# Edge keys decoded one turn ahead of their gather, with four buffers for indices and segment masks

## The chip, the cores and the metric

The kernel runs on one core of a Trainium2 chip. The metric is device time of the whole kernel in microseconds. Engines are named as in the profile: PE (TensorE), DVE (VectorE), ACT (ScalarE), POOL (GpSimd), SP (SyncE).

## The reference

The input is a batch of images, 128 channels of 32 x 32, that is 32768 tokens of 128 values for each of two halves. A convolution block with binarised weights comes first. Then a graph attention layer over 524288 random edges plus one self edge for each token sets the gates of a mixture of four experts:

```
h = (x_flat @ W_gat).reshape(M, HEADS, NUM_EXPERTS)          # 4 heads, 4 experts
e = leaky_relu(a_src[src] + a_dst[dst], 0.2)
ee = exp(e - segment_max(e, dst)[dst]);  denom = segment_sum(ee, dst)
agg = segment_sum(h[src] * (ee / denom[dst])[:, :, None], dst)
... layernorm, mean over heads, top 2 of 4, softmax ...
out = sum over experts of gate * (gelu(x @ W1[ei] + b1[ei]) @ W2[ei] + b2[ei])
```

What matters here is the middle: for every edge one row `h[src]` of 24 floats has to be fetched, and maxima, sums and products have to be run along edges sorted by their destination.

## The kernel before

The kernel has four stages, one after the other: `sorter` sorts the edges by destination (the first 1078 us, on DVE), `mixer` does the convolution block and writes the rows of `h` to memory, `attention` walks the sorted edges, and `finish_lower` collects the sums for each token and finishes the first half of the images. The change is in `attention` alone.

`attention` lays the 557056 sorted entries out as 128 partitions of 4352 and walks them in `CHUNKS` = 64 chunks of `COLS` = 68 columns. Five engines run the same loop, `rounds(eng, 6, LAST, 3, 4, body)`, over 65 turns k; each calls its own `body(k, at, turn)`, and semaphores alone keep them in step. `at` is the turn's number within the unrolled loop, so that `at % 2` and `at % 4` name buffers.

One turn k of DVE, in program order (DVE works strictly in this order):

1. Decode of chunk k (L788 to L811): it waits for the key load, splits the packed keys into a segment number `seg`, the source row `index` (L799; after it `idx` is signalled, L800) and three masks `start`, `cont`, `cut`. Before L799 it waits (L798) until the gather of chunk k-2 has landed, because `index` has two buffers. Each instruction waits for the one before (`go`).
2. In turns 0 to 3 a quarter of the expert gates of the other half, `x.weigh_vector` (L814; its instructions are at L1113 to L1150), and in turn 0 also `x.start_vector`.
3. Four small instructions that split the targets for a histogram (L821 to L825).
4. Attend to chunk k-1 (L843 to L872): it waits for the gather of chunk k-1 (`gat`, L843). The first part (L848 to L862) makes the running maximum and the differences `dif`; ACT takes their exponentials (L770); the second part (L864 and 20 scans at L870) makes the running sums `out`, and signals `out` (L872).
5. The experts' share (`Experts.vector`, L1336): the output of the tile before (L1345), and then eight steps, each one product with the gate (`ex_hs`, L1351) and one group of 8 column pairs for the histogram: `one_hot` (L876 to L881) writes `is_lo` (L879) and `is_hi` (L880), 16 instructions a group, 128 a turn.

POOL, turn k (L735 to L740): it waits for `idx` of chunk k and for `out` of chunk k-2 (the buffer `got` has two places), and then issues 68 gathers (indirect DMAs), one for each column, 128 rows of 96 bytes each.

PE, turn k (`Experts.tensor`, L1284): 16 steps. In the first eight it multiplies `ex_hs` with the second weights (L1296), makes the next hidden values (L1250) and then the histogram matmuls of that step's group (L751), for which it waits on `one_hot`. The last eight steps are the other half's tile (`ex_kept_ps`, L1301), for which nothing of DVE is needed. ACT makes the GELUs (L1332) and the copies of the kept outputs (L1324) in the same order; the exponentials of turn k+1 (L770) come after all of them in ACT's program.

SP, turn k: it stores `out` of chunk k-1 (L713, after `out`), loads the keys (L718, after the decode of chunk k) and targets of chunk k+2, and moves the experts' tiles.

What orders the work around the change is therefore the program order of DVE, and two semaphores on POOL:

```
need(pool, S["idx"], k + 1)      # L735: indices of chunk k
need(pool, S["out"], k - 1)      # L736: sums of chunk k-2
```

Of the kernel before, what the change touches and what calls it, by code (L numbers as in the profile page):

```python
# [666 lines left out]
def attention(nc, edges_d, keys_d, rows_d, res_d, agg, half, gathers, make_experts=None, finish=None):  # L667
    with ExitStack() as ctx, ExitStack() as during:
        def keep(name, shape, dt=F32): return ctx.enter_context(nc.sbuf_tensor(f"e{half}_{name}", shape, dt))
        def sb(name, shape, dt=F32): return during.enter_context(nc.sbuf_tensor(f"e{half}_{name}", shape, dt))  # L670
# [24 lines left out]
        def decodes(k): return not isinstance(k, int) or k < CHUNKS  # L695
# [6 lines left out]
        with nc.Block() as block:  # L702
# [24 lines left out]
            @block.gpsimd  # L727
            def _(pool):
                pool.iota(iota_i[:, :], [[1, HIS]], base=0, channel_multiplier=0).then_inc(S["iot"], 1)
                if x: x.start_gpsimd(pool)  # L730
                pool.wait_ge(S["edge"], 1)
                pool.indirect_dma_start(head0[:, :], None, rows_d, bass.IndirectOffsetOnAxis(ap=first[:, :], axis=0)).then_inc(S["head"], 16)
                def body(k, at, turn):
                    if decodes(k):
                        need(pool, S["idx"], k + 1)  # L735
                        need(pool, S["out"], k - 1)  # L736
                        pool.sem_inc(S["free"], 1)
                        for c in range(COLS):
# [36 lines left out]
            def _(v):  # L775
                v.wait_ge(S["iot"], 1)
                v.tensor_copy(iota_f[:, :], iota_i[:, :]).then_inc(S["iot"], 1)
                v.tensor_copy(iota_b[:, :], iota_i[:, :]).then_inc(S["iot"], 1)

                def body(k, at, turn):  # L780
                    if decodes(k):
                        u = at % 2
                        i = [0]
                        def go(ins):
                            i[0] += 1
                            ins.then_inc(S["dec"], 1)
                            v.wait_ge(S["dec"], DEC * k + i[0])
                        v.wait_ge(S["key%d" % u], 16 * (at // 2 + 1) + 32 * turn)  # L788
                        kk = key[:, u, :]
                        go(v.tensor_scalar(sgn[:, :], kk, 31, None, ALU.arith_shift_right))  # L790
                        go(v.tensor_tensor(mag[:, :], kk, sgn[:, :], ALU.bitwise_xor))
                        go(v.tensor_scalar(low[:, :], mag[:, :], 16, None, ALU.logical_shift_right))
                        go(v.scalar_tensor_tensor(out=seg[:, :], in0=sgn[:, :], scalar=float(FLIP), in1=low[:, :], op0=ALU.mult, op1=ALU.add))
                        go(v.tensor_scalar(dfull[:, :], seg[:, :], float(SHIFT + HALF * half), None, ALU.add))
                        go(v.tensor_tensor(mag[:, :], mag[:, :], dfull[:, :], ALU.bitwise_xor))
# [5 lines left out]
                        go(v.tensor_tensor(start[:, u, :], seg[:, 1:COLS+1], seg[:, 0:COLS], ALU.not_equal))  # L801
                        go(v.tensor_scalar(cont[:, u, :], start[:, u, :], -1.0, 1.0, ALU.mult, ALU.add))
                        go(v.tensor_scalar(cut[:, u, :], start[:, u, :], -BIG, None, ALU.mult))
                        if isinstance(k, int) and k == 0:
                            go(v.tensor_copy(prev_seg[:, :], seg[:, 0:1]))
                            go(v.tensor_copy(first_seg[:, :], seg[:, 1:2]))
                            v.tensor_scalar(first[:, :], dfull[:, 1:2], 65535, None, ALU.bitwise_and).then_inc(S["edge"], 1)
                        else:
                            go(v.tensor_copy(last_seg[:, :], seg[:, COLS:COLS+1]))
                            go(v.tensor_copy(last_seg[:, :], seg[:, COLS:COLS+1]))  # L810
                        assert i[0] == DEC  # L811

                        if x and isinstance(k, int) and k < x.WEIGHINGS:
# [14 lines left out]
                    if attends(k):  # L828
                        q = (at - 1) % 2
                        j = k - 1  # L830
# [4 lines left out]
                        def settle():  # L835
                            v.wait_ge(S["proc"], PROC * j + i[0])
# [10 lines left out]
                        by_head = lambda ap: ap.unsqueeze(1).broadcast_to([P, HEADS, COLS])  # L847
                        go(v.tensor_tensor(adv[:, :, :], g[:, :, 20:24].rearrange("p c h -> p h c"), by_head(start[:, q, :]), ALU.mult)); settle()  # L848
                        for h in range(HEADS):
                            go(v.tensor_tensor_scan(ad[:, q, h, :], cont[:, q, :], adv[:, h, :], ad[:, 1 - q, h, COLS-1:COLS], ALU.mult, ALU.add))  # L850
                        settle()
# [3 lines left out]
                        for h in range(HEADS):  # L855
                            go(v.tensor_tensor_scan(mx[:, q, h, 1:COLS+1], cut[:, q, :], e[:, h, :], mx[:, 1 - q, h, COLS:COLS+1], ALU.add, ALU.max))
                        settle()
                        go(v.tensor_tensor(dif[:, 0, :, :], mx[:, q, :, 0:COLS], by_head(cut[:, q, :]), ALU.add)); settle()
                        go(v.tensor_tensor(dif[:, 0, :, :], dif[:, 0, :, :], mx[:, q, :, 1:COLS+1], ALU.subtract))
# [6 lines left out]
                        for h in range(HEADS):  # L866
                            for w in range(EXPERTS + 1):
                                ch = h * EXPERTS + w if w < EXPERTS else HEADS * EXPERTS + h
                                data = wgt[:, h, w, :] if w < EXPERTS else rp[:, 1, h, :]
                                go(v.tensor_tensor_scan(out[:, q, :, ch], rp[:, 0, h, :], data, out[:, 1 - q, COLS-1, ch:ch+1], ALU.mult, ALU.add))  # L870
# [748 lines left out]
```

## Time and profile before

| | us |
|---|---|
| median of 3 runs | 10095.95 (10090.94 to 10100.3) |
| span of the profiled execution | 10069.6 |
| median minus span (launch and end, and the spread of runs) | 26.4 |

| engine | busy us | share |
|---|---|---|
| DVE | 5609.3 | 56% |
| POOL | 5042.1 | 50% |
| PE | 4088.4 | 41% |
| ACT | 1868.9 | 19% |

The profiled execution stands for itself: its span is the time from its first to its last instruction, and the 26.4 us are what the median of the timed runs has beyond it. The profile is one execution's; a row of it gives an engine, a line of the kernel, an operation, the tiles it writes and reads, and times. `attention` takes the span from about 2132 to 9454 us, so it is nearly three quarters of the kernel.

### The profile page before, as it was taken

Reading aid. Unit: us, or ns where it says so; the run is one execution under the profiler, and the core shown is the slowest. Engines: PE = TensorE matmul, PEld = TensorE weight load, DVE = VectorE, ACT = ScalarE, POOL = GpSimd, SP = SyncE. Lnnn points to the kernel's source line nnn. Section 1 sums busy time; section 2 is a strip of 40 time slices with the busy share of each in tenths; the row PEclk is TensorE's granted clock in tenths of the full one; section 3 lists DMA queues with packets and bytes.
Section 4 is the critical chain, followed back from the end, with each engine's and each line's share of the span. In section 5 each row is a group of like instructions: output and inputs, shape, how many; then the busy total and the mean of one; then the engine's idle time right before and its main releaser. Section 6 shows DMA issues by size and latency. Waiting matters only on the chain. (4 is left out here: it accounts for less than half of the span.)

```text
span 10069.6 us, 67922 instructions
## 1 busy us (share of the span) xinstructions
PE 4088.4 (41%) x14109; PEld 1997.0 (20%) x14171; DVE 5609.3 (56%) x16515; ACT 1868.9 (19%) x3239; POOL 5042.1 (50%) x4836
## 2 busy tenths in 40 slices
PE   0011388833344444434444444344444444334233
PEld 0010255521111111112111111111111121111100
DVE  9999788845444444444444444444444444444388
ACT  0000377721111111111111111111111111111111
POOL 0000155545566556665656556665666556665452
PEclk9855688866676777677776777667776777667655
DMA  0000133311111111111111111111111111111156
GB/s 17 0 0 0 55 120 118 120 46 31 31 44 32 31 31 36 39 32 31 32 43 32 31 31 35 40 32 31 31 44 32 31 31 35 40 32 27 44 191 199
DMA packets 351386, 467.68 MB, mean 46 GB/s; under 512 B 176559, under 2 KB 252290, under 8 KB 334338
## 3 DMA queue, kind: packets, MB, share of 16 engines
q1 hardware_dynamic: 203562, 408.25, 11.6%
q0 software_dynamic: 147552, 56.95, 5.9%
q14 instruction: 241, 1.97, 0.1%
q8 instruction: 31, 0.51, 0.0%
HBM read 234.91 MB, written 229.93 MB: 46 GB/s over the span
## 5 line engine op out<-in xcount | busy, mean ns | idle before, releaser
L739 POOL DMA_INDIRECT e_got<-rows,e_index x4352 | 4285.0, 985 | 2982.4 <-DVEq L800 1674.8
L751 PE MATMUL e_count_ps<-e_is_hi,e_is_lo 128*128 128x256 bf16 x4096 | 699.1, 328 | 3044.3 <-DMA keys<-s_u_b 2348.6
L879 DVE TENSOR_SCALAR e_is_lo<-e_iota_b,e_tlo 128x128 bf16<-128x128 bf16 x4096 | 1057.3, 258 | 1534.1 <-issue 1174.2
L880 DVE TENSOR_SCALAR e_is_hi<-e_iota_b,e_thi 128x256 bf16<-128x256 bf16 x4096 | 1184.2, 290 | 1247.4 <-issue 1247.2
L1332 ACT ACTIVATE ex_hh<-ex_hid_ps,ex_b 128x512 f32<-128x512 f32 x1024 | 696.7, 687 | 5889.8 <-remote 2776.9
L751 PEld LDWEIGHTS e_count_ps<-e_is_hi,e_is_lo 128*128 128x128 bf16 x4096 | 426.0, 114 | 3391.5 <-DMA keys<-s_u_b 2419.4
L1296 PE MATMUL ex_out_ps<-ex_hs,ex_w 128*128 128x512 f32 x1024 | 757.8, 832 | 18.1 <-remote 11.4
L1250 PE MATMUL ex_hid_ps<-ex_tn,ex_w 128*128 128x512 f32 x1024 | 661.3, 734 | 0.0
L1301 PE MATMUL ex_kept_ps<-ex_hh,ex_w 128*128 128x512 f32 x1024 | 542.1, 611 | 273.2 <-ACT ex_kept L1324 187.4
L864 DVE TENSOR_TENSOR e_wgt<-e_got,e_rp 128x1088 f32<-128x1088 f32 x64 | 180.5, 2820 | 681.1 <-issue 499.9
L180 POOL MEMSET m_identb<- 128x128 bf16 x1 | 0.2, 205 | 1077.7 <-POOLq L85 1077.7
L1250 PE MATMUL ex_hid_ps<-ex_lower,ex_w 128*128 128x512 f32 x1024 | 522.9, 592 | 0.0
L1351 DVE TENSOR_TENSOR ex_hs<-ex_hh,ex_gate_ps 128x512 f32<-128x512 f32 x512 | 348.3, 680 | 171.3 <-issue 169.4
L1291 PE MATMUL ex_out_ps<-ex_turned,ex_b 36*128 36x512 bf16 x64 | 38.5, 601 | 891.4 <-DVE ex_o L1345 454.8
L384 ACT ACTIVATE m_xt<-m_ln_ps,m_nb,m_rs 128x128 f32<-128x128 f32 x1024 | 370.6, 466 | 31.6 <-DVE m_nb L326 31.6
L1470 POOL DMA_INDIRECT c_trow<-sums,c_tidx x256 | 260.2, 1017 | 188.9 <-DVE c_tidx L1520 96.1
L1250 PEld LDWEIGHTS ex_hid_ps<-ex_tn,ex_w 128*128 128x128 f32 x1024 | 260.9, 255 | 377.6 <-issue 372.4
L207 POOL TENSOR_TENSOR m_xm<-m_out,m_xin 128x1024 f32<-128x1024 f32 x64 | 151.4, 2366 | 362.5 <-issue 303.4
L654 PE MATMUL s_turned<-s_ident,s_ping 128*128 128x128 f32 x288 | 54.9, 379 | 674.8 <-DVEq L546 674.8
L235 PE MATMUL m_conv_ps<-m_sg,m_w1T 128*128 128x512 bf16 x1152 | 318.8, 439 | 5.9 <-DVE m_z L349 5.9
L870 DVE TENSOR_TENSOR_SCAN e_out<-e_rp,e_out,e_wgt 128x68 f32<-128x68 f32 x1024 | 289.8, 364 | 28.2 <-issue 24.1
L1301 PEld LDWEIGHTS ex_kept_ps<-ex_hh,ex_w 128*128 128x128 f32 x1024 | 173.7, 189 | 554.5 <-ACT ex_hh L1332 284.2
(358 smaller groups left out, 6435.0 us busy)
## 6 DMA issues: line engine op xcount, KB each, us to landing
e_got<-rows,e_index POOLq DMA_INDIRECT x4352
kept<-ex_kept SPq DMA_DIRECT2D x64, 1024.0 KB
c_kept<-kept SPq DMA_DIRECT2D x64, 1024.0 KB
sums<-e_out SPq DMA_DIRECT2D x64, 816.0 KB
m_xin<-in_x_dram SPq DMA_DIRECT2D x64, 512.0 KB, 4.6
mid<-m_xm SPq DMA_DIRECT2D x64, 512.0 KB, 2.9
norm<-m_tn SPq DMA_DIRECT2D x64, 512.0 KB, 4.7
ex_tn<-norm SPq DMA_DIRECT2D x64, 256.0 KB
```

The costliest lines, as they stand in the source:

```text
L235: last = pe.matmul(conv_ps[:, hf*512:(hf+1)*512], w1T[:, t, :], sg1[:, at % 2, hf*rows_of+dy:hf*rows_of+dy+rows_of, dx:dx+W], start=(t == ...
L384: last = act.activation(xt[:, b*P:(b+1)*P], src[:, b*P:(b+1)*P], ACT.Identity, bias=nb[:, b:b+1], scale=rs[:, b:b+1])
L739: pool.indirect_dma_start(got[:, at % 2, c, :], None, rows_d, bass.IndirectOffsetOnAxis(ap=index[:, at % 2, c:c+1], axis=0)).then_inc(S["g ...
L751: last = pe.matmul(count_ps[:, 0:HIS], is_lo[:, g % 2, t, :], is_hi[:, g % 2, t, :], start=(isinstance(k, int) and k == 0 and g == 0 and t ...
L870: go(v.tensor_tensor_scan(out[:, q, :, ch], rp[:, 0, h, :], data, out[:, 1 - q, COLS-1, ch:ch+1], ALU.mult, ALU.add))
L879: v.tensor_scalar(is_lo[:, g % 2, t, :], iota_b[:, 0:P], tlo[:, n:n+1], None, ALU.is_equal)
L880: last = v.tensor_scalar(is_hi[:, g % 2, t, :], iota_b[:, :], thi[:, n:n+1], None, ALU.is_equal)
L1250: pe.matmul(self.hid_ps[:, s % 2, :], self.w1[:, e, f*P:(f+1)*P], tokens[:, at % 4, :], start=True, stop=True).then_inc(S["w1"], 1)
L1296: pe.matmul(self.out_ps[:, :], self.w2[:, e, f, :], self.hs[:, s % 2, :], start=False, stop=(s == self.GATED - 1)).then_inc(S["w2"], 1)
L1301: pe.matmul(self.kept_ps[:, :], self.w2[:, e, f, :], self.hh[:, s % 2, :], start=(f == 0), stop=(f == HID - 1)).then_inc(S["w2"], 1)
L1332: act.activation(self.hh[:, s % 2, :], self.hid_ps[:, s % 2, :], ACT.Gelu, bias=self.b1[:, s % self.GATED // HID, s % HID:s % HID + 1]).th ...
L1351: v.tensor_tensor(self.hs[:, s % 2, :], self.hh[:, s % 2, :], self.gate_ps[:, (s // HID) % 2, :], ALU.mult).then_inc(S["mul"], 1)
```

## The change

The decode becomes a function `decode(k, at, turn)`. It is called once before the loop for chunk 0, and then at the head of turn k for chunk k+1. `index`, `start`, `cont` and `cut` get four buffers (`at % 4`); the wait of the decode for the gather of chunk k-2 is gone. POOL's gather reads `index[:, at % 4, ...]`, and the attending part reads the masks of its own chunk, k-1. A loop variable `w` is renamed `lane`. Nothing else changes: not POOL's two waits, nor the order of steps 2 to 5 on DVE.

```diff
-        index = sb("index", [P, 2, COLS], I32); first = sb("first", [P, 1], I32)
-        start = sb("start", [P, 2, COLS]); cont = sb("cont", [P, 2, COLS]); cut = sb("cut", [P, 2, COLS])
+        index = sb("index", [P, 4, COLS], I32); first = sb("first", [P, 1], I32)
+        start = sb("start", [P, 4, COLS]); cont = sb("cont", [P, 4, COLS]); cut = sb("cut", [P, 4, COLS])
...
-                                bass.IndirectOffsetOnAxis(ap=index[:, at % 2, c:c+1], axis=0)).then_inc(S["gat%d" % (at % 4)], 16)
+                                bass.IndirectOffsetOnAxis(ap=index[:, at % 4, c:c+1], axis=0)).then_inc(S["gat%d" % (at % 4)], 16)
...
+                def decode(k, at, turn):
+                    u, w = at % 2, at % 4
...
+                    v.wait_ge(S["key%d" % u], 16 * (at // 2 + 1) + 32 * turn)
...
+                    go(v.tensor_scalar(index[:, w, :], mag[:, 1:COLS+1], 65535, None, ALU.bitwise_and))
+                    v.sem_inc(S["idx"], 1)
+                    go(v.tensor_tensor(start[:, w, :], seg[:, 1:COLS+1], seg[:, 0:COLS], ALU.not_equal))
+                    go(v.tensor_scalar(cont[:, w, :], start[:, w, :], -1.0, 1.0, ALU.mult, ALU.add))
+                    go(v.tensor_scalar(cut[:, w, :], start[:, w, :], -BIG, None, ALU.mult))
...
+                decode(0, 0, 0)
                 def body(k, at, turn):
+                    if not isinstance(k, int) or k + 1 < CHUNKS:
+                        decode(k + 1, at + 1, turn)
                     if decodes(k):
                         u = at % 2
...
-                        if not isinstance(k, int) or k >= 2:
-                            v.wait_ge(S["gat%d" % ((at - 2) % 4)], 16 * COLS * ((at - 2) // 4 + 1) + 16 * COLS * turn)
-                        go(v.tensor_scalar(index[:, u, :], mag[:, 1:COLS+1], 65535, None, ALU.bitwise_and))
-                        v.sem_inc(S["idx"], 1)
...
-                        q = (at - 1) % 2
+                        q, w = (at - 1) % 2, (at - 1) % 4
...
-                        go(v.tensor_tensor(adv[:, :, :], g[:, :, 20:24].rearrange("p c h -> p h c"), by_head(start[:, q, :]), ALU.mult)); settle()
+                        go(v.tensor_tensor(adv[:, :, :], g[:, :, 20:24].rearrange("p c h -> p h c"), by_head(start[:, w, :]), ALU.mult)); settle()
```

## Rows read from the trace of the kernel before

**Rows 1.** The page, parts 1 and 5: busy time by engine; the gathers.
```profile
PE 4088.4 (41%) x14109; PEld 1997.0 (20%) x14171; DVE 5609.3 (56%) x16515; ACT 1868.9 (19%) x3239; POOL 5042.1 (50%) x4836
...
L739 POOL DMA_INDIRECT e_got<-rows,e_index x4352 | 4285.0, 985 | 2982.4 <-DVEq L800 1674.8
```

**Rows 2.** Waits of POOL: total us, times, longest.
```profile
POOL e_got L739 <- DVEq L800: 1674.8, 63, 39.9
```

**Rows 3.** One turn cut into stretches: length, busy us of each engine, clock, DMA.
```profile
4552.10:4556.20 4.10, 3.93 (x16) 2.14 (x16) 3.24 (x18) 0.96 (x2) 1.19 (x2) 1.00 0.00 0
4556.20:4574.00 17.80, 11.64 (x26) 4.31 (x24) 6.13 (x16) 7.81 (x12) 13.60 (x14) 1.00 0.10 10
4574.00:4582.30 8.30, 0.00 (x0) 0.00 (x0) 7.97 (x21) 2.54 (x3) 7.01 (x5) 0.60 0.07 7
4582.30:4590.30 8.00, 7.22 (x17) 2.89 (x18) 7.25 (x32) 0.69 (x1) 6.17 (x7) 0.57 0.64 210
4590.30:4643.00 52.70, 13.07 (x32) 5.10 (x30) 12.41 (x39) 1.37 (x2) 39.73 (x43) 0.62 0.17 37
4643.00:4650.90 7.90, 3.49 (x11) 2.08 (x12) 0.00 (x0) 0.00 (x0) 0.00 (x0) 0.51 0.02 2
4650.90:4665.50 14.60, 12.16 (x49) 6.04 (x48) 13.69 (x68) 3.44 (x5) 0.00 (x0) 0.88 0.00 1
```

**Rows 4.** Timeline of that turn: first gather; end of ACT's tile; second attending part.
```profile
4554.71 0.95 POOL L739 DMA_INDIRECT e_got<-rows,e_index  x1 [27.30 <-DVEq L800]
...
4571.31 0.69 ACT L1324 ACTIVATE ex_kept<-ex_kept_ps,ex_b2c 128x512 f32<-128x512 f32 x1 [3.00 <-issue]
...
4574.00 2.82 DVE L864 TENSOR_TENSOR e_wgt<-e_got,e_rp 128x1088 f32<-128x1088 f32 x1 [10.96 <-ACT e_rp L770]
4574.07 3.49 POOL L739 DMA_INDIRECT e_got<-rows,e_index  x1 [0.30 <-issue]
...
4582.34 0.69 DVE L1345 TENSOR_TENSOR ex_o<-ex_xm,ex_out_ps 128x512 f32<-128x512 f32 x1 [0.33 <-DVE e_out L870]
```

**Rows 5.** Timeline later in that turn: two one-hots; a group's end, and PE's answer.
```profile
4608.86 0.28 DVE L880 TENSOR_SCALAR e_is_hi<-e_iota_b,e_thi 128x256 bf16<-128x256 bf16 x1 [1.03 <-issue]
4610.26 0.25 DVE L879 TENSOR_SCALAR e_is_lo<-e_iota_b,e_tlo 128x128 bf16<-128x128 bf16 x1 [1.11 <-issue]
...
4638.26 0.29 DVE L880 TENSOR_SCALAR e_is_hi<-e_iota_b,e_thi 128x256 bf16<-128x256 bf16 x1 [1.14 <-issue]
...
4647.41 1.89 PE L751 MATMUL e_count_ps<-e_is_hi,e_is_lo 128*128 128x256 bf16 x8 [17.38 <-DMA keys<-s_u_b]
```

**Rows 6.** Gather starts (turns 0, 1, 21, finish) up to DVE's slowing, columns as rows 3.
```profile
2137.70:2164.00 26.30, 0.00 (x0) 0.00 (x0) 21.11 (x45) 4.61 (x5) 20.07 (x21) 0.50 0.11 10
2255.90:2290.60 34.70, 13.23 (x29) 4.89 (x28) 20.97 (x37) 9.88 (x14) 26.41 (x28) 0.82 0.09 9
4554.70:4590.30 35.60, 20.36 (x46) 7.77 (x45) 22.45 (x75) 11.72 (x16) 27.97 (x26) 0.81 0.21 54
9495.60:9587.00 91.40, 0.00 (x0) 0.00 (x0) 15.11 (x39) 2.65 (x3) 69.00 (x72) 0.50 0.22 62
```

**Rows 7.** Timeline of turn 2: attending late beside a gather, first and last.
```profile
2428.27 0.82 DVE L848 TENSOR_TENSOR e_adv<-e_got,e_start 128x272 f32<-128x272 f32 x1 [2.50 <-DMA s_u_a<-keys]
...
2476.78 0.69 DVE L1345 TENSOR_TENSOR ex_o<-ex_xm,ex_out_ps 128x512 f32<-128x512 f32 x1 [6.84 <-remote]
```

**Rows 8.** Timeline of turn 1: the gates' first and last instruction.
```profile
2256.34 1.22 DVE L1113 TENSOR_TENSOR ex_cen<-agg,ex_con 128x1024 f32<-128x1024 f32 x1
...
2294.82 0.56 DVE L1150 COPY parts<-parts 128x768 bf16<-128x768 bf16 x1 [1.04 <-DVE parts L1150]
```

**Rows 9.** Lines L790, L1345, L879: durations ns, first and last start.
```profile
L790 DVE TENSOR_SCALAR e_sgn<-e_key x64: 178/183/200, 2132.1 to 9314.4; 128x69 int32<-128x69 int32 x64
L1345 DVE TENSOR_TENSOR ex_o<-ex_xm,ex_out_ps x64: 686/687/690, 2351.7 to 9454.1; 128x512 f32<-128x512 f32 x64
L879 DVE TENSOR_SCALAR e_is_lo<-e_iota_b,e_tlo x4096: 233/247/504, 2195.2 to 9424.6; 128x128 bf16<-128x128 bf16 x196
```

More of the change, by code:

```diff
@@ L778, in _, with go @@
                 v.tensor_copy(iota_b[:, :], iota_i[:, :]).then_inc(S["iot"], 1)
+                def decode(k, at, turn):
+                    u, w = at % 2, at % 4
+                    i = [0]
+                    def go(ins):
+                        i[0] += 1
+                        ins.then_inc(S["dec"], 1)
+                        v.wait_ge(S["dec"], DEC * k + i[0])
+                    v.wait_ge(S["key%d" % u], 16 * (at // 2 + 1) + 32 * turn)
+                    kk = key[:, u, :]
+                    go(v.tensor_scalar(sgn[:, :], kk, 31, None, ALU.arith_shift_right))
+                    go(v.tensor_tensor(mag[:, :], kk, sgn[:, :], ALU.bitwise_xor))
+                    go(v.tensor_scalar(low[:, :], mag[:, :], 16, None, ALU.logical_shift_right))
+                    go(v.scalar_tensor_tensor(out=seg[:, :], in0=sgn[:, :], scalar=float(FLIP), in1=low[:, :], op0=ALU.mult, op1=ALU.add))
+                    go(v.tensor_scalar(dfull[:, :], seg[:, :], float(SHIFT + HALF * half), None, ALU.add))
+                    go(v.tensor_tensor(mag[:, :], mag[:, :], dfull[:, :], ALU.bitwise_xor))
+                    go(v.tensor_scalar(index[:, w, :], mag[:, 1:COLS+1], 65535, None, ALU.bitwise_and))
[3 more added lines that the diff above has]
+                    go(v.tensor_scalar(cut[:, w, :], start[:, w, :], -BIG, None, ALU.mult))
+                    if isinstance(k, int) and k == 0:
+                        go(v.tensor_copy(prev_seg[:, :], seg[:, 0:1]))
+                        go(v.tensor_copy(first_seg[:, :], seg[:, 1:2]))
+                        v.tensor_scalar(first[:, :], dfull[:, 1:2], 65535, None, ALU.bitwise_and).then_inc(S["edge"], 1)
+                    else:
+                        go(v.tensor_copy(last_seg[:, :], seg[:, COLS:COLS+1]))
+                        go(v.tensor_copy(last_seg[:, :], seg[:, COLS:COLS+1]))
+                    assert i[0] == DEC
@@ L780, in body @@
+                decode(0, 0, 0)
                 def body(k, at, turn):
+                    if not isinstance(k, int) or k + 1 < CHUNKS:
+                        decode(k + 1, at + 1, turn)
                     if decodes(k):
                         u = at % 2
[L783 to L794, printed above, removed]
@@ L795, in body @@
-                        go(v.tensor_tensor(mag[:, :], mag[:, :], dfull[:, :], ALU.bitwise_xor))
-                        if not isinstance(k, int) or k >= 2:
-                            v.wait_ge(S["gat%d" % ((at - 2) % 4)], 16 * COLS * ((at - 2) // 4 + 1) + 16 * COLS * turn)
-                        go(v.tensor_scalar(index[:, u, :], mag[:, 1:COLS+1], 65535, None, ALU.bitwise_and))
-                        v.sem_inc(S["idx"], 1)
-                        go(v.tensor_tensor(start[:, u, :], seg[:, 1:COLS+1], seg[:, 0:COLS], ALU.not_equal))
@@ L802, in body @@
[L802 to L810, printed above, removed]
@@ L811, in body @@
-                        assert i[0] == DEC
                         if x and isinstance(k, int) and k < x.WEIGHINGS:
@@ L847, in body @@
                         by_head = lambda ap: ap.unsqueeze(1).broadcast_to([P, HEADS, COLS])
-                        go(v.tensor_tensor(adv[:, :, :], g[:, :, 20:24].rearrange("p c h -> p h c"), by_head(start[:, q, :]), ALU.mult)); settle()
+                        go(v.tensor_tensor(adv[:, :, :], g[:, :, 20:24].rearrange("p c h -> p h c"), by_head(start[:, w, :]), ALU.mult)); settle()
                         for h in range(HEADS):
-                            go(v.tensor_tensor_scan(ad[:, q, h, :], cont[:, q, :], adv[:, h, :], ad[:, 1 - q, h, COLS-1:COLS], ALU.mult, ALU.add))
+                            go(v.tensor_tensor_scan(ad[:, q, h, :], cont[:, w, :], adv[:, h, :], ad[:, 1 - q, h, COLS-1:COLS], ALU.mult, ALU.add))
                         settle()
@@ L855, in body @@
                         for h in range(HEADS):
-                            go(v.tensor_tensor_scan(mx[:, q, h, 1:COLS+1], cut[:, q, :], e[:, h, :], mx[:, 1 - q, h, COLS:COLS+1], ALU.add, ALU.max))
+                            go(v.tensor_tensor_scan(mx[:, q, h, 1:COLS+1], cut[:, w, :], e[:, h, :], mx[:, 1 - q, h, COLS:COLS+1], ALU.add, ALU.max))
                         settle()
-                        go(v.tensor_tensor(dif[:, 0, :, :], mx[:, q, :, 0:COLS], by_head(cut[:, q, :]), ALU.add)); settle()
+                        go(v.tensor_tensor(dif[:, 0, :, :], mx[:, q, :, 0:COLS], by_head(cut[:, w, :]), ALU.add)); settle()
                         go(v.tensor_tensor(dif[:, 0, :, :], dif[:, 0, :, :], mx[:, q, :, 1:COLS+1], ALU.subtract))
@@ L866, in body @@
                         for h in range(HEADS):
-                            for w in range(EXPERTS + 1):
-                                ch = h * EXPERTS + w if w < EXPERTS else HEADS * EXPERTS + h
-                                data = wgt[:, h, w, :] if w < EXPERTS else rp[:, 1, h, :]
+                            for lane in range(EXPERTS + 1):
+                                ch = h * EXPERTS + lane if lane < EXPERTS else HEADS * EXPERTS + h
+                                data = wgt[:, h, lane, :] if lane < EXPERTS else rp[:, 1, h, :]
                                 go(v.tensor_tensor_scan(out[:, q, :, ch], rp[:, 0, h, :], data, out[:, 1 - q, COLS-1, ch:ch+1], ALU.mult, ALU.add))
```

## The prediction, as it stood before the result

> **What bounds the kernel now.** I read the page first. No engine is full: DVE is busy for 56% of the span and POOL for 50% [rows 1]. The largest single group is POOL's 4352 gathers, and ahead of them POOL stood idle for 1674.8 us, in 63 waits for the indices that DVE's decode signals [rows 1, 2]: 26.6 us a turn. That is what the change aims at. Whether it is worth anything depends on what DVE does while POOL gathers, so I cut one turn (chunk 21) into stretches [rows 3]. A turn is 113.4 us there, and DVE's program runs through it in order:
>
> - 4.1 us: decode and target split, 18 instructions.
> - 17.8 us: first attending part, of which 11.0 us are a wait for ACT's exponentials [rows 4]. ACT comes late because its half of the kept tile ends only at 4572.0, 20 us after DVE's last one-hot. So 6.8 us are work.
> - 8.3 us: second attending part. At its end `out` is signalled.
> - 83.2 us: the experts' share with the 128 one-hots, 139 instructions in all (32 + 39 + 0 + 68). This part I call H. At DVE's full rate (68 instructions in 13.69 us busy, 4.97 per us) it would take 28 us.
>
> The gather of a turn starts 2.6 us into it, at 4554.7, and ends at 4643, 88.3 us long. For its first 36 us DVE runs beside it at full rate: 32 instructions in 8.0 us between 4582.3 and 4590.3. Then something gives way: 39 instructions in 60.6 us, 1.55 us each, two neighbours 1.4 us apart though each is busy for 0.25 to 0.29 us, and PE sees the end of a group 8.9 us late (4638.55 to 4647.41) [rows 3, 5]. This lasts until 4650.9, 7.9 us after the last gather; then DVE is fast at once. So a turn is bounded by neither POOL nor DVE alone: gather start + 96 us of which 60 are nearly lost, and after it the 14.6 us of one-hots that are left, and only then the next decode and the next gather.
>
> **The change, part by part.** *Buffers and the wait that goes.* The wait for the gather of chunk k-2 never ended late: the attending part of turn k-1 had waited for that gather already. Worth 0. The renamed variable: 0.
>
> *The decode moved ahead.* The same 12 instructions, once a turn; one extra call before the loop. It needs the keys of chunk k+1 at the head of turn k. SP issues that load after `out` of turn k-1, as before, and H lies between, 28 us at the least; so 0, and SP passes no other queue. Queued behind the key wait on DVE would be the whole turn, but nothing makes it late.
>
> *When POOL starts.* Of its two waits, `idx` of chunk k is now there a turn early, and `out` of chunk k-2 becomes the one that ends last: it is signalled at the end of attending in turn k-1. The gather of chunk k thus starts at the head of H in turn k-1, not after the decode in turn k. POOL stays one gather in each turn, and its idle time does not go: it waits for `out` in place of `idx`.
>
> *What lies beside the gather.* Before: decode, attending with its 11 us wait, then H. Now: H first, then the next decode, then attending. Both orders have the same DVE work, so the question is how much of it is done before DVE slows. The onsets in the trace [rows 6]: 26.3 us after the gather's start in turn 0, 34.7 in turn 1, 35.6 in turn 21, but with 21.1, 21.0 and 22.5 us of DVE busy time in each. In the finishing stage 72 gathers ran in 91.4 us with 15.1 us of DVE and no slowing. I take 21 us of DVE work beside a gather as the allowance; DVE's waits do not use it up. By instructions (45, 37, 75) or by gathers (21, 28, 26) the same rows agree less well or not with the finishing stage; these are rivals below.
>
> Count from the gather's start T = 0, the head of H. 21 us at 4.97 per us: 104 of 139 instructions. The other 35 at 1.55 us: 54 us, T+75. The next decode, 18 instructions at 1.4 us, is 25 us, cut off where the slowing ends at T+96: done at T+97. First attending part 6.8 us: T+104. The exponentials need ACT's 20 us of kept tile, begun at T+75: if it runs at full rate there is no wait and attending ends at T+112, if it stands still until T+96 it ends at T+124. I take the middle and a little less, P = 115 us a turn, because PE and ACT post fewer signals than DVE. Before it is 113.4. The 11 us wait used to lie in the fast part of a gather and be covered by nothing else; what is saved of it is paid back by 12 us more of slow stretch (75 for 61 us).
>
> *The ends* [rows 7 to 9]. Turn 0: gathers 0 and 1 run back to back, 2 x 88 us, so the slowing lasts until about 188 us after the decode at 2132.1. H starts at 63 us (first one-hot 2195.2): 125/1.55 = 81 instructions, then 58 fast, 12 us: turn 0 takes 200 us. Turn 1 up to its `out`: 4.1 + 38.5 (gates, with their waits) + 6.8 + 8.3 = 58. Turns 2 and 3: 96 + 38.5 + 6.8 + 8.3 = 150 each. Then 60 turns of P. At the end H without a gather and one attending with its wait, 28 + 26 = 54. Sum 612 + 60 P. Before, from the first decode to the last L1345, it is 9454.1 - 2132.1 = 7322. With P = 115: 7512, so 190 us more; break-even is P = 111.8. The profiled span becomes 10260, and with the 26.4 us that the median has beyond the span, 10286 us.
>
> *A rule weighed.* Beside the 2.82 us product of two SBUF operands (L864) a gather took 3.49 us in place of 0.95, and it started first on neither side by more than 0.07 us [rows 4]; beside the fast one-hots gathers kept nearly their rate, 7 in 8.0 us, and DVE its own [rows 3]. The Trainium skill (SBUF — State Buffer, "Who interferes with whom") has one rule for both: VectorE and GpSimd share one port pair under an exclusive lock, so that a tensor_scalar in a two-port mode and a GpSimd instruction block each other fully. It speaks against this change, which puts all one-hots beside gathers. For L864 the trace agrees; for the one-hots it agrees from 4590 on at best and not in the 8 us before. By the rule every one-hot would be slow from the gather's start, which is the far end of rival A.
>
> **The rivals.**
>
> A. *The one-hots use up the allowance faster than their busy time, and H becomes the bound* (slower). They come at 4.97 per us, where the attending parts have about 2.6. If the allowance is a number of instructions, it is 37 to 75 [rows 6]: gone after 7 to 15 us. Then by T+96 52 to 57 more are done, 12 to 45 are left, H ends at T+98 to T+105, and decode, attending and the whole wait follow in the open, 30.2 us: P = 129 to 135. With none fast: 96/1.55 = 62 done, 77 left, 15.5 us, P = 142. It decides where fewer than about 85 of the 139 run before the onset. For it: the slowing is paid per instruction (1.4 us whatever its length). Against it: 37 against 75 is no constant. Time: 60 x 129 + 612 - 7322 = 1030 more, 11126; at 135, 11486.
>
> B. *The onset goes by gathers or by time, and H fits before it* (faster). 21 to 28 gathers are 26 to 35 us. H (28) and the decode (4) end at T+32; attending runs slowly, 48.5 us as in turn 2 [rows 7], so `out` comes at T+81 and the next gather starts at T+88, when POOL is free; with some of the next H beside the end of the old one P is about 95. If the onset is at 25 us, 15 instructions of H are slow (T+48), the decode (T+73), the first attending part, 21 us as in turn 2 up to L864, T+94, and the second is fast: P = 104. For it: 26.3 to 35.6 us is a narrow spread. Against it: the finishing stage, 72 gathers without onset. Time: 9090 to 9630.
>
> C. *The change doesn't do what it says*: `out` hides the early indices in a way that leaves the turn as it was, P = 112. Time 60 x 112 + 612 - 7322 = 10 more, 10106. Only the phase of the gather could spare it.
>
> **How the numbers follow.** The forecast 0.45 (P 110 to 120, its own range 9990 to 10590), A 0.22, B 0.30, C 0.03. A measurement tells about 0.2%, 20 us, from no change. Of the forecast's 0.45, 0.08 lies below 10076 (P under 111.5) and 0.04 within 20 us. Faster: 0.30 + 0.08 = 0.38. Same: 0.04 + 0.03 = 0.07. Slower: 0.33 + 0.22 = 0.55. The range leaves out the fast half of B with its price under 9500 and the far end of A over 11150, together about 2 in 10.
>
> **What would show it.** Right: POOL's wait ahead of L739 is no longer on L800 but on DVE's L872, still about 25 us a turn; the first gather of a turn starts within 1 us of L1345; one-hots are fast for about 20 us after it, then 1.4 us apart; L864 waits for ACT only briefly. Turn 0 is near 200 us. Wrong: a fast H to its end and slow scans at L870 (B), slow one-hots within 15 us of L1345 and L864 waiting 11 us (A), or two gathers without a gap in the steady turns.

## The result, and the profile after

The changed kernel takes 11572.6 us (median of 4 runs, 11562.8 to 11579.6) against 10094.1 us before on the same chip: ratio 1.146, 95% interval 1.1445 to 1.1478. It is slower by 1479 us, outside the range that was given.

The page of the changed kernel (busy time by engine; gathers; one-hots; the experts' activation) and three rows of its waits (total us, times, longest):

```profile
PE 4234.9 (37%) x14109; PEld 2062.7 (18%) x14171; DVE 5410.4 (47%) x16515; ACT 1860.6 (16%) x3239; POOL 4873.6 (42%) x4836
...
L739 POOL DMA_INDIRECT e_got<-rows,e_index x4352 | 4117.4, 946 | 4592.1 <-DVEq L875 3285.0
L882 DVE TENSOR_SCALAR e_is_lo<-e_iota_b,e_tlo 128x128 bf16<-128x128 bf16 x4096 | 1068.1, 261 | 2868.4 <-remote 2143.1
...
L1335 ACT ACTIVATE ex_hh<-ex_hid_ps,ex_b 128x512 f32<-128x512 f32 x1024 | 689.9, 686 | 7464.5 <-remote 4328.7
```
```profile
ACT ex_hh L1335 <- remote: 4328.7, 180, 36.5
POOL e_got L739 <- DVEq L875: 3285.0, 62, 87.7
DVE e_is_lo L882 <- remote: 2143.1, 160, 21.1
```

Beside [rows 1, 2]: POOL's wait has moved from the decode (1674.8 us) to the signal `out` (3285.0 us, 53 us each time). It did not go, it doubled. The largest wait on the list is ACT's, and it was so before the change as well, at two thirds of the size. The prediction did not read this row. Below it, from [rows 3]'s turn, ACT's longest idle time (its product was ready at 4605.80, PE's L1250):

```profile
ACT ex_hh L1332 <- remote: 2776.9, 130, 33.6
...
4631.36 0.69 ACT L1332 ACTIVATE ex_hh<-ex_hid_ps,ex_b 128x512 f32<-128x512 f32 x1 [32.90 <-remote]
```

One steady turn of the changed kernel from the first gather, cut as [rows 3]: to the end of the fast start; to the end of the slow stretch; rest of H; decode and target split; attending. Columns as there.

```profile
4746.90:4756.00 9.10, 8.74 (x24) 3.74 (x25) 9.10 (x44) 0.69 (x1) 6.91 (x8) 0.63 0.90 305
4756.00:4842.60 86.60, 17.90 (x51) 7.90 (x48) 12.00 (x47) 2.06 (x3) 57.31 (x61) 0.58 0.10 12
4842.60:4852.40 9.80, 6.76 (x24) 3.66 (x24) 9.78 (x50) 1.95 (x3) 0.00 (x0) 0.66 0.00 0
4852.40:4856.20 3.80, 3.80 (x16) 2.04 (x16) 3.04 (x17) 1.11 (x2) 0.00 (x0) 1.00 0.00 0
4856.20:4883.60 27.40, 12.34 (x27) 4.50 (x25) 14.73 (x39) 10.60 (x15) 0.04 (x1) 0.87 0.00 0
```

The turn is 136.7 us (113.4 in [rows 3]). The gather is no longer than before, 84.7 us. What has grown is the time without a gather, 52 us in place of 25: rest of H, decode, and all of attending lie in it. The time comes out of the prediction's own sum with this turn: 60 x 136.5 (the mean turn) + 612 - 7322 = 1480 us more.

What the slow stretch is made of stands in the timeline (start, length, instruction, idle time before it). These are the third product of the turn on PE, ready at 4758.17, ACT's step before it, free at 4759.18, ACT's answer to the product, and DVE's answer to ACT:

```profile
4757.15 1.02 PE L1253 MATMUL ex_hid_ps<-ex_tn,ex_w 128*128 128x512 f32 x2
...
4758.49 0.69 ACT L1335 ACTIVATE ex_hh<-ex_hid_ps,ex_b 128x512 f32<-128x512 f32 x1 [6.05 <-PE ex_hid_ps L1253]
...
4786.63 0.69 ACT L1335 ACTIVATE ex_hh<-ex_hid_ps,ex_b 128x512 f32<-128x512 f32 x1 [27.45 <-issue]
4790.05 0.69 DVE L1354 TENSOR_TENSOR ex_hs<-ex_hh,ex_gate_ps 128x512 f32<-128x512 f32 x1 [5.88 <-remote]
```

ACT stands idle for 27.45 us with product and buffer ready (the buffer's last reader on DVE was done at 4754.85) and nothing else to do; DVE starts 2.7 us after ACT's end. The turn's first product was ready at 4751.63, and ACT started at 4751.75. The profile puts most of these waits down to `remote` or `issue`, which names no engine, so the end of whatever an instruction needs has to be looked up in the timeline.

This can be done for every hand-over of H, in the turns whose H starts between 3000 and 8000 us. An instruction's lateness is its start minus the later of two times: when its engine was free, and when what it needs had ended. The longest, in us:
```
                           before  changed  e8 (below)
PE's product to ACT          27.4     36.5     40.6
PE's histogram to DVE        10.6     21.1     22.0
DVE's one-hots to PE         10.1     11.0      0.1
ACT's GELU to DVE             1.1      2.8      2.7
```
So the lateness goes by the producer. It is long behind PE, and behind DVE where DVE ran a group of 16 one-hots just before.

### The profile page after: what moved, and what is told of

Its sections match the earlier page's. It is cut to its first block and busy times, and to the rows that moved or that the text cites. A ratio compares the mean times of both kernels' runs of the same rounds, so it can differ in the third digit from the quotient of the medians.

```text
span 11561.1 us, 67889 instructions
## 1 busy us (share of the span) xinstructions
PE 4234.9 (37%) x14109; PEld 2062.7 (18%) x14171; DVE 5410.4 (47%) x16515; ACT 1860.6 (16%) x3239; POOL 4873.6 (42%) x4836
## 5 line engine op out<-in xcount | busy, mean ns | idle before, releaser
L739 POOL DMA_INDIRECT e_got<-rows,e_index x4352 | 4117.4, 946 | 4592.1 <-DVEq L875 3285.0
L751 PE MATMUL e_count_ps<-e_is_hi,e_is_lo 128*128 128x256 bf16 x4096 | 771.1, 352 | 4131.7 <-DMA keys<-s_u_b 1972.3
L751 PEld LDWEIGHTS e_count_ps<-e_is_hi,e_is_lo 128*128 128x128 bf16 x4096 | 463.2, 122 | 4533.7 <-DMA keys<-s_u_b 2008.6
L1299 PE MATMUL ex_out_ps<-ex_hs,ex_w 128*128 128x512 f32 x1024 | 819.7, 896 | 391.0 <-issue 262.2
L1253 PE MATMUL ex_hid_ps<-ex_lower,ex_w 128*128 128x512 f32 x1024 | 546.8, 616 | 0.0
L867 DVE TENSOR_TENSOR e_wgt<-e_got,e_rp 128x1088 f32<-128x1088 f32 x64 | 180.5, 2820 | 737.0 <-ACT e_rp L770 736.6
L1299 PEld LDWEIGHTS ex_out_ps<-ex_hs,ex_w 128*128 128x128 f32 x1024 | 227.9, 275 | 472.6 <-issue 283.7
L1241 DVE COPY ex_turned<-ex_turned_ps 36x512 bf16<-36x512 bf16 x64 | 26.7, 417 | 607.7 <-remote 480.0
```

The source lines that it names most:

```text
L751: last = pe.matmul(count_ps[:, 0:HIS], is_lo[:, g % 2, t, :], is_hi[:, g % 2, t, :], start=(isinstance(k, int) and k == 0 and g == 0 and t ...
L1253: pe.matmul(self.hid_ps[:, s % 2, :], self.w1[:, e, f*P:(f+1)*P], tokens[:, at % 4, :], start=True, stop=True).then_inc(S["w1"], 1)
L1299: pe.matmul(self.out_ps[:, :], self.w2[:, e, f, :], self.hs[:, s % 2, :], start=False, stop=(s == self.GATED - 1)).then_inc(S["w2"], 1)
```

## The experiments

Before on the same chip: 10027 us for e1 to e4, 10020 for e5 to e8, 10083 for e9 to e12, 10087 for e13 to e16, 10095 for e17 and e18. Ratios with 95% intervals; e8, e13, e14 are one run each, e2 to e4 two. T is the start of a turn's gathers.

**e1, the phase of the gather alone.** The decode stays a turn ahead, the gather starts where it did before.
```
 decode(k + 1, ...)              # head of turn k
+v.sem_inc(S["go"], 1)
 ...
+need(pool, S["go"], k + 1)      # POOL, ahead of chunk k's gathers
```


> The changed kernel with one more wait: POOL issues the gather of chunk k only after DVE has passed the head of turn k, just behind the decode of chunk k+1. So the decode stays a turn ahead and the four buffers stay, and only the start of the gather goes back to where it was. Theory PHASE (the loss comes from where in DVE's turn the gather lies, the one-hots now being at its head): the turn is 113 us again and the time 10050 to 10150. Rival BODY (the decode ahead, its code or its buffers cost by themselves): it stays near 11570.

10076 us, 1.0051 (1.0031 to 1.0071). So 14% of the 14.6% are the phase; decoding ahead with four buffers, with the added signal, costs 0.5%.

**e2, a phase between.** `go` is released ahead of the turn's sixth group of one-hots (`g == 5`).


> The changed kernel with the gather of chunk k+1 released inside the experts' share of turn k, behind its fifth group of one-hots: 48 one-hots lie at the head of the gather, then decode and attending. PHASE with an allowance of about 45 one-hot instructions (onset 9 to 11 us after the gather's start, as in the changed kernel): attending runs slowly, about 48 us, to T+64, then about 12 one-hots in 32 us, the rest after T+96: turn about 115, 10200. PHASE with an allowance by DVE busy time of 21 us: turn 105 to 107, about 9650. BODY: near 11570.

10671 us, 1.064 (turns of 112 to 132 us): above what either allowance gave (10200 and 9650) and well under BODY. The later in H the gather starts, the less is lost.

**e3, e4, another form of one-hot, changed order.** e3 reads `iota_f` in place of `iota_b`; e4 writes a group's 16 one-hots with two broadcast `tensor_tensor`.


> The changed kernel with the one-hots compared from the fp32 iota in place of the bf16 one; output, count and order of instructions are the same. Theory PORT (the slowing comes from the one-hots' bf16 mode, which takes something that the gathers need): the share with the one-hots takes about 40 us at full rate beside the gather, the turn falls to about the gather's 88 us, 8700 to 9200. Rival COUNT (each DVE instruction costs, whatever its mode): onset after about 45 instructions as before, turn 136 or a little more, 11550 to 11900.

> The changed kernel with the 16 one-hot instructions of a group made by two (8 columns at once by broadcast), the same elements written. COUNT: 34 instructions in the experts' share in place of 139, so it fits before the onset or loses little: turn 88 to 103, 8700 to 9650. A theory of DVE busy time (21 us): onset at the sixth group, turn about 103, 9650. PORT or a theory of written elements: the onset comes as early as now and the turn stays over 120, above 10600.

e3: 10617 us, 1.0586, between the ranges of PORT and COUNT. Every second H now ran fast to its end beside the gathers (139 instructions by T+35), which refutes both the allowance by instructions and the one by 21 us of busy time. The next H, behind two gathers in a row, was slow until 16 us after the last. e4: 10142 us, 1.0113, in no range of its three theories either (its H has 27 instructions, and not the 34 of the expectation). In both DVE holds POOL back. These are the first gathers of e3 beside float32 one-hots (1.48 and 1.54 us apart; in the changed kernel 1.25), and three of e4 beside the broadcast ones:

```profile
4607.82 0.94 POOL L739 DMA_INDIRECT e_got<-rows,e_index  x1 [0.30 <-issue]
4609.06 1.17 POOL L739 DMA_INDIRECT e_got<-rows,e_index  x1 [0.30 <-issue]
4610.54 1.23 POOL L739 DMA_INDIRECT e_got<-rows,e_index  x1 [0.30 <-issue]
4612.08 1.06 POOL L739 DMA_INDIRECT e_got<-rows,e_index  x1 [0.30 <-issue]
```
```profile
4597.72 3.95 POOL L739 DMA_INDIRECT e_got<-rows,e_index  x1 [0.30 <-issue]
4601.97 3.64 POOL L739 DMA_INDIRECT e_got<-rows,e_index  x1 [0.30 <-issue]
4605.91 3.67 POOL L739 DMA_INDIRECT e_got<-rows,e_index  x1 [0.30 <-issue]
```

I saw this only as a delay of POOL; that this may be what keeps H fast I saw only with e9.

**e5, SP's transfers.** SP waits for the end of H before it issues tile stores and loads.
```
-need(sp, S["fin"], k)
+need(sp, S["hdone"], k)         # DVE signals it after the last one-hot
```


> The changed kernel, but SP issues a token tile's output store, the next tile's three loads and the kept store only after the last one-hot of the turn (DVE signals it), not at the head of H; the sums store and the loads of keys and targets stay. In both kernels the time of the first slow one-hot also lies 8 to 9 us behind the start of SP's transfers (before: packets from 4582, onset at 4590; after: packets from 4747, onset at 4756), because both come with H. TRANSFERS (the SP transfers bring on the slow stretch): the one-hots stay fast to their end at about T+30, the onset moves behind the late transfers, period 95 to 115 us, time 9000 to 10300. ENGINES (it comes from DVE's own instructions beside the gathers): onset at T+9 to T+11 as before, H ends near T+105, period 134 to 140, time 11450 to 11750.

11464 us, 1.1442 (1.1423 to 1.1461), turns of 134 to 137 us: TRANSFERS is refuted.

**e6, e7, the other one-hots in the old order.** The edits of e4 and e3 on the kernel before.


> The kernel before, with each group's 16 one-hots as two broadcast tensor_tensor instructions (16 per turn in place of 128). PER-INSTRUCTION (what is lost in the slow stretch is 1.4 us an instruction): H of 27 instructions ends inside the gather, the turn is bounded by the gather plus decode, 2.6 + 88 + 3 to 10 us, period 94 to 105, time 9000 to 9700. PORT (the rate of DVE beside gathers is set by how long it works): the wide instructions carry the same elements, the turn stays 108 to 116, time 9800 to 10250.

> The kernel before, with one-hots that read the float32 iota in place of the bfloat16 one. Beside a gather's start the float32 one-hots of the changed order ran all 128 without slowing. FORM (bfloat16 one-hots bring the slow stretch on early): here the onset at 36 us after the gather's start goes away or moves past the end of H at about T+60, period 92 to 102, time 8800 to 9500. AGE (the slow stretch comes once gathers have run for 30 to 50 us with DVE busy): onset at T+36 to T+48 as before, period 105 to 116, time 9600 to 10250.

e6: 9934 us, 0.9916 (0.99 to 0.9933). e7: 10088 us, 1.0072, turns of 113.5 us on average, onset at T+33 to T+50. PER-INSTRUCTION and FORM are refuted: an eighth of the one-hots' instructions buys 0.8%, and the form nothing. Both times lie in the ranges of PORT and AGE, which had little change to forecast.

**e8, few one-hots.** `for t in range(RING)` becomes `range(1)` in the one-hots, after the first two groups of the first chunk.


> The changed kernel with only one pair of one-hots in each group in place of eight (16 per turn in place of 128; the other tiles keep what the first chunk left, so the counts are not the reference's). PER-INSTRUCTION: H of 27 instructions is done by about T+35 whatever its rate, the gathers go on without long gaps, period 85 to 105, time 8400 to 9700. If instead the period stays above 120, the 128 one-hots are not what the turn waits for, and PE's and ACT's late signals are.

11388 us, a turn of 133.8 us. This felled what the prediction and all experiments so far had taken for granted. One turn, first 9.1 us and slow stretch, then the fourth product of the turn on PE, ready at 4717.45, ACT's step before it, and its answer to the product; last, three starts on DVE and PE:

```profile
4703.90:4713.00 9.10, 8.78 (x28) 3.85 (x29) 3.40 (x11) 0.69 (x1) 6.96 (x8) 0.71 0.91 305
4713.00:4799.30 86.30, 17.32 (x54) 7.28 (x52) 3.97 (x11) 2.75 (x4) 57.30 (x61) 0.60 0.09 12
```
```profile
4716.43 1.02 PE L1253 MATMUL ex_hid_ps<-ex_tn,ex_w 128*128 128x512 f32 x2
...
4725.05 0.69 ACT L1335 ACTIVATE ex_hh<-ex_hid_ps,ex_b 128x512 f32<-128x512 f32 x1 [11.25 <-remote]
4759.34 0.69 ACT L1335 ACTIVATE ex_hh<-ex_hid_ps,ex_b 128x512 f32<-128x512 f32 x1 [33.61 <-remote]
```
```profile
4748.07 0.25 DVE L882 TENSOR_SCALAR e_is_lo<-e_iota_b,e_tlo 128x128 bf16<-128x128 bf16 x1 [19.61 <-remote]
...
4760.06 0.69 DVE L1354 TENSOR_TENSOR ex_hs<-ex_hh,ex_gate_ps 128x512 f32<-128x512 f32 x1 [11.44 <-issue]
...
4760.81 2.08 PE L1299 MATMUL ex_out_ps<-ex_hs,ex_w 128*128 128x512 f32 x2 [10.24 <-DVE ex_hs L1354]
```

DVE has 11 instructions in 86.3 us and the stretch is as long as with 47. So DVE's instructions are not what H waits for, but the hand-overs that go round PE, ACT and DVE eight times: here ACT answers PE's product 33.6 us after it was free, and DVE answers a group of PE's histogram, done at 4715.7, 19.6 us after it was free. The next hand-overs come without delay: ACT ends at 4760.03, DVE starts at 4760.06 and ends at 4760.75, PE starts at 4760.81. What is late comes from PE. A round of PE has 24 to 32 matmuls and weight loads, and e8 left them all. Whether a late hand-over costs time by the signal, or by the instructions that PE (or DVE, with 16 one-hots) ran before it, no run here tells: none changed PE's number.

**e9 to e12, room between the gathers.** One or two small instructions on POOL after each gather.
```
 pool.indirect_dma_start(...)
+for r in range(N):              # N = 1 (e9, e11) or 2 (e10, e12)
+    last = pool.memset(pause[:, c, r:r+1], 0.0)
 ...                             # last signals `rest`; POOL's next chunk waits for it
```


> The changed kernel with one 128x1 POOL memset after every gather, so that the gathers leave POOL about 1.41 us apart in place of 1.25. PACE (whatever serves the gathers behind POOL needs some 1.37 us for one, so at 1.25 us apart they pile up; signals of all engines then come late, until the pile is worked off: 8 us after one chunk of 68, 16 us after two chunks in a row, both 0.12 us a gather): at 1.41 us nothing piles up, the 8 rounds of H between PE, ACT and DVE take 30 to 35 us as they do at a gather's start, the gathers follow one another almost without a gap, 68 x 1.41 = 96 us, period 96 to 102, time 9050 to 9550. ENGINES (it comes from DVE's instructions beside any running gather): onset near T+10, the slow stretch longer because the gathers last 96 us, period 145 to 150, time 12000 to 12400.

> The same with two 128x1 memsets after every gather: about 1.57 us apart. PACE: no late signals either, period 68 x 1.57 = 107 to 112 us, time 9700 to 10100, so slower than with one memset. ENGINES: period 155 to 160, time 12600 to 13000.

> The kernel before with one 128x1 POOL memset after every gather. PACE: H runs fast, about 30 us, and ends near T+60, beside the gather; the next decode follows at once and POOL goes on without a gap, period 96 to 102, time 9050 to 9550. ENGINES: the turn is lengthened by the longer gather, 113 + 11 = 124 us, time 10700 to 10900.

> The kernel before with two memsets after every gather. PACE: period 107 to 112, time 9700 to 10100. ENGINES: 113 + 22 = 135 us, time 11300 to 11600.

Changed order: 11313 us (1.1225) and 10879 us (1.0786). Old order: 9812 us (0.973) and 9402 us (0.9323; 0.9307 to 0.9338). More work for POOL made both kernels faster, so ENGINES is refuted. PACE had the direction, and its range held in none of the four (e12 came out faster than it): the gathers were not evenly wider apart. POOL of e10, memsets between gathers, and one pause of 1.5 us:

```profile
4702.25 0.94 POOL L740 DMA_INDIRECT e_got<-rows,e_index  x1 [0.18 <-issue]
4703.19 0.11 POOL L743 MEMSET e_pause<- 128x1 f32 x1
4703.46 0.10 POOL L743 MEMSET e_pause<- 128x1 f32 x1 [0.16 <-issue]
4705.07 0.94 POOL L740 DMA_INDIRECT e_got<-rows,e_index  x1 [1.51 <-issue]
4706.02 0.14 POOL L743 MEMSET e_pause<- 128x1 f32 x2
4706.32 0.94 POOL L740 DMA_INDIRECT e_got<-rows,e_index  x1 [0.16 <-issue]
```

**e13, half the gathers.** `range(COLS)` becomes `range(COLS // 2)` on POOL from the third chunk on, and the counts waited for are halved.


> The changed kernel with 34 of a chunk's 68 gathers from the third chunk on (the other columns keep older rows, so its numbers are not the reference's). The gathers last 42.5 us in place of 85. BOUND TO THE END (H's signals stay late until some 10 us after the last gather, and then the last three rounds take 10 us): H ends near T+63, attending 31 us behind it, period 94, time 11560 - 60 x 42.5 = about 9010. BY ROUNDS (each of H's signals costs its time whatever is left of the gathers): H ends at T+75 or later, period 106 to 112, time 9700 to 10100. INSTRUCTIONS (the prediction's own arithmetic: 46 fast, the rest 1.55 us apart while it lasts): 46 + 28 = 74 by T+53, 65 left, 13 us: T+66, period 97, near the first.

8847 us, a turn of 92.4 us (9010 and 94 expected). Its four stretches, cut as in the changed kernel (fast start; slow; rest of H; decode and attending):

```profile
4748.30:4757.40 9.10, 8.79 (x23) 3.81 (x24) 9.10 (x44) 0.69 (x1) 6.96 (x8) 0.62 0.89 289
4757.40:4796.40 39.00, 9.22 (x34) 4.39 (x33) 7.92 (x29) 1.38 (x2) 25.22 (x27) 0.60 0.11 21
4796.40:4809.90 13.50, 12.39 (x44) 5.46 (x42) 13.50 (x68) 3.17 (x5) 0.00 (x0) 0.88 0.00 0
4809.90:4840.60 30.70, 15.57 (x40) 6.46 (x40) 17.68 (x55) 11.30 (x16) 0.00 (x0) 0.89 0.00 0
```

H ends at T+61.7, 19 us after the last gather; in the changed kernel at T+105.5, 21 us after it. That fits BOUND TO THE END and refutes BY ROUNDS: in these two kernels a turn is the length of its gathers and 50 to 52 us. INSTRUCTIONS (T+66, 97 us) lies only 5 us off; what speaks against it is e8. DVE was slow for 5.7 us after the last of 34 gathers, 9 to 11 after 68, 16 after 136 in a row (e3).

**e14 to e16, more room.** N = 4 in the changed order, N = 3 in the old one, N = 2 with the broadcast one-hots of e6.


> The changed kernel with four 128x1 memsets after each gather, about 1.65 us from gather to gather. With one H ended at T+101, with two at T+78. PACE: the signals are no longer late, H ends at T+35 to T+45, the gathers of 112 us follow one another with hardly a gap, period 112 to 116, time 10000 to 10250. ENGINES: the late signals stay, H ends near T+80 or later, period 140 and more, over 11600.

> The kernel before with three memsets after each gather, about 1.5 us from gather to gather. PACE: H ends beside the gather, period 68 x 1.5 = 102 to 106 us, time 9350 to 9600, about that of two memsets (9402), which ended 16 of 128 one-hots behind the gather. ENGINES: period over 110, time over 9800.

> The kernel before with two memsets after each gather and each group's one-hots as two broadcast instructions. Alone these took 6.8% and 0.8%. PACE: both shorten H beside the gather, the gathers (1.40 us apart) follow without a gap, period 96 to 101, time 9050 to 9350. If the broadcast instructions block POOL (they delayed gathers to 1.7 to 2.2 us apart), the gather becomes longer, period 103 to 110, time 9400 to 9800.

e14: 9179 us, 0.91 of before, under the range expected. e15: 9189 us, 0.9105 (0.909 to 0.9121), under its range too. e16: 9818 us, 0.9736, at the end of the range for gathers held up: the broadcast one-hots hold POOL up and take back more than half of what the pace gives. The gathers of e14 on the page, its longest wait for a signal, and a turn of 99.6 us from the start of H, which lies 15 us after the first gather (H and decode; wait for the gather; attending):

```profile
L740 POOL DMA_INDIRECT e_got<-rows,e_index x4352 | 4262.9, 980 | 907.1 <-issue 681.6
```
```profile
ACT ex_hh L1339 <- remote: 2756.2, 444, 12.3
```
```profile
4652.50:4702.20 49.70, 30.43 (x106) 14.06 (x107) 32.49 (x145) 4.81 (x7) 41.84 (x173) 0.81 0.25 70
4702.20:4736.90 34.70, 18.68 (x32) 6.80 (x30) 1.75 (x11) 8.52 (x12) 26.68 (x117) 0.75 0.08 9
4736.90:4752.10 15.20, 0.00 (x0) 0.00 (x0) 14.26 (x37) 3.21 (x4) 12.79 (x46) 0.61 0.07 8
```

All 139 instructions of H pass beside the gathers, ACT's tile too, and attending no longer waits for the exponentials. POOL goes from chunk to chunk without a gap (569 gathers in 840 us): now, and only now, it is the bound, and the change does what it was drawn for. ACT's longest `remote` wait is still 12.3 us, and not 36.5.

**e17, e18, what the room must look like.** e17: twelve memsets after each eighth gather, none after the others. e18: N = 3, changed order.


> The changed kernel with twelve 128x1 memsets after every eighth gather, none after the others: about 1.7 us of pause in 10 us, the other gathers 1.25 us apart as in the changed kernel. PAUSES (signals get through while POOL is not in a gather, so that one pause in eight gathers serves all): H ends by T+50, the gathers run on, period 97 to 105, time 9000 to 9500. SPACING (each gather needs a little more room): the signals stay late between the pauses, H ends at T+75 to T+100, period 125 to 140, time 10800 to 11700.

> The changed kernel with three memsets after each gather, the pace that gave 9189 us in the old order. With two the changed order still waited (10879 us), with four it did not (9179 us). If the order does not matter once the signals get through, it is POOL-bound at 98 to 102 us a turn and takes 9100 to 9300; if the changed order needs more room because all of H lies at the head of the gather, H ends past T+50, a gap opens before some gathers, and it takes 9400 to 10500.

e17: 10018 us, 0.9916 (0.9894 to 0.9937). H ends at T+48 to T+74, and a turn is 98 to 127 us, mostly near 115. Between both theories: pauses help much, but four memsets after each gather do more. e18: 9666 us, 0.956 (0.9523 to 0.9597), against 0.9105 for the same pace in the old order (e15). This is in the second of the ranges expected: the changed order needs more room.

The changed order in one table (us, steady turns; spacing is the mean from gather to gather in a chunk; H begins with the chunk's first gather, in e14 15 us after it, so that it ends at T+62 there):
```
                 memsets  spacing   H lasts  mean turn
changed kernel        0    1.25        106     136.5
e9   one             68    1.38        101     132.6
e10  two            136    1.41         78     126.2
e17  12 to eight     96    1.42      49-74     114.0
e18  three          204    1.42      54-61     107.7
e14  four           272    1.45      45-50     100.2
```
The mean spacing hardly differs from e9 to e18, and H becomes 43 us shorter: it is not the mean rate that decides. Nor is it how often POOL has something else to do: e17 has fewer memsets than e10, in 8 places of a chunk in place of 68, and a shorter H. What in POOL's pauses decides stays open.

## Why the prediction was wrong

- **Where POOL starts, and what it waits for:** right in kind. The gather starts within 1 us of L1348, POOL waits on `out`, one gather to a turn. In size wrong: 53 us in place of about 25.
- **The failed step: "104 of 139 instructions" of H beside the gather, H done at T+75.** In 50 steady turns 45 to 54 instructions ran before the first slow one, which started at T+11 to T+13 (in two turns at T+23), and H ended at T+105. The allowance of 21 us of busy time came from three onsets in [rows 6] that lie within 1.5 us of each other. That was a coincidence: in e3 a whole H passed, and in e8 the slow stretch began after 11 instructions of 3.4 us.
- **Beneath it: "35 at 1.55 us".** 1.55 us was the mean of [rows 3] over waits for signals and instructions 1.4 us apart, taken as the price of an instruction. e8 shows that it is none: what the stretch lasts is set by hand-overs from PE, up to 36.5 us late in the changed kernel. [Rows 5] had the other reading, PE 8.9 us late, and I used it for nothing; in [rows 7] DVE's L1345 waited 6.84 us for a remote signal; and ACT's wait of 2776.9 us stood first in the list of waits before.
- **"PE and ACT post fewer signals than DVE", so the exponentials' wait is half covered:** wrong. ACT waited longest of all, began the kept tile only after the slow stretch, and the wait at L867 is 12.0 us, against 11.0 before. The sum of that passage is off as well: 75 for 61 us is 14 us more of slow stretch, and not 12.
- **The end of the slowing at T+96, turn 0 of 200 us, the ends and the sum:** right. DVE is fast again at T+95.7, turn 0 takes 200.8 us from its first gather (205.7 from the first decode). With the measured turn the sum gives 8802 us from the first decode to the last L1348, and the profile has 8821.
- **The rivals.** A's far end nearly came true (H at T+98 to T+105, 30.2 us in the open; measured T+105 and 31.2; a turn of 129 to 135, measured 136.5), and so did its two signs, but by another mechanism than it named: that is luck. It had 0.22, and the range cut it at 11150. B and C fell.
- **The rule weighed** (the Trainium skill, SBUF — State Buffer, "Who interferes with whom"): for the float32 and broadcast one-hots the traces agree as far as POOL is held up, with gathers 1.5 us apart beside the one and 3.6 to 3.95 us long beside the other; beside the bfloat16 `tensor_scalar` ones gathers stayed 1.25 us apart. The same section says that "PE and ACT never wait on anyone". Here ACT started 27.45 us late, and 33.6 us in e8, while POOL gathered; if that concerns ports alone, it says nothing of signals.

**Shown and open.** Shown: the loss is the phase (e1, e2); it is not SP's transfers (e5), nor DVE's instructions (e8); H ends 19 and 21 us after the last of 34 and of 68 gathers (e13); what POOL does between gathers changes how late the hand-overs are (e9 to e18; the longest from PE to ACT falls from 36.5 to 11.8 us in e14). Argued only: that DVE's blocking of POOL kept H fast in e3 for the same reason, and so did L864 before, whose gather took 3.49 us [rows 4] 13 us ahead of the onset; in e3 the first late signal came some 14 us after POOL's last blocked gather. Open: which path the hand-overs share with the gathers; whether they cost by the signal or by the instruction that PE ran before; and why DVE's own instructions, with no wait between them, are 1.4 us apart in that time.

## What to carry to other kernels

Before work is moved beside a long run of indirect gathers, count the hand-overs between engines in it, and what the producer ran before each, not the consumer's instructions alone: in the changed kernel they came up to 36 us late behind PE and up to 11 behind DVE, until some 10 us after the last gather. A mean time per instruction taken from a stretch with waits in it is no price; look in the timeline for who finished when and who answered when. And try room between the gathers first: three small POOL instructions after each took 9% off the kernel before, without any change of order. The changed order with four gave the same (9179 and 9189 us), with three less (9666 us); four in the old order were not run.

## What the runs showed of the hardware that was not expected

- Hand-overs from PE up to 36.5 us late beside gathers 1.25 us apart, with the DMA engines 10% busy; from ACT at most 2.8 us; from DVE up to 11.0 us behind 16 one-hots and at most 0.6 us behind two (e4, e8).
- More instructions on POOL made the program faster: 17408 memsets of 0.12 us, and 21% less time (11573 to 9179 us, on chips whose kernel before differed by 0.1%).
- After N memsets to a gather the gathers do not come evenly later: most are 1.25 to 1.30 us apart, and 8 to 11 of a chunk's 68 are followed by one only after 1.5 to 3 us or a little more (e9, e10, e18, e14).
- A wait of 11.3 us in the slow stretch was followed by 11 one-hots at full rate before the next slow one.
